# Three phases per step, two banks each for the score tiles, and the node columns read from an SBUF ring, in a graph layer with POOL-issued row moves

## The reference

```python
proj = einsum('ni,rio->nro', x, relation_weight)
t_r, h_r = proj[src, etype], proj[dst, etype]
att = sum(t_r * tanh(h_r + efeat), axis=-1)
a = segment_softmax(att, dst)
h_nb = segment_sum(x[src] * a[:, None], dst, n)
out = leaky_relu((x + h_nb) @ W.T, 0.01) + leaky_relu((x * h_nb) @ W2.T, 0.01)
return layernorm(x + out)
```

## Time and profile before

| | |
|---|---|
| median of 3 runs | 765.6 us |
| span of the profiled execution | 908.0 us |
| PE, DVE busy | 642.8 us, 608.1 us |
| POOL, ACT busy | 572.8 us, 514.2 us |
| DMA, mean | 77 GB/s |

### The profile page before, as it was taken

How to read it: one execution, slowest core, us unless ns; L and a number is a source line. 1 busy time by engine, 2 the same in 40 slices (tenths; PEclk the granted TensorE clock), 3 DMA queues, 4 the chain that set the end, 5 groups by cost and what they waited for, 6 DMA issues and landing times. The chain is left out here.

```text
span 908.0 us, 13811 instructions
## 1 busy us (share of the span) xinstructions
PE 642.8 (71%) x3948; PEld 356.0 (39%) x3948; DVE 608.1 (67%) x1094; ACT 514.2 (57%) x1457; POOL 572.8 (63%) x594
## 2 busy tenths in 40 slices
PE   2587778877777877877887876877788778865030
PEld 1434343544443443443443443343344344344020
DVE  2459768778778868869778769865686567754050
ACT  0255575577677667767677677744455244555052
POOL 7466666666666666666666666666666666666726
PEclk9788988798998998999897989879987889786555
DMA  5332432333332432432432421321111110000000
GB/s 139 107 101 71 115 103 81 114 103 81 115 103 81 116 104 69 127 103 67 128 104 60 123 81 45 104 73 64 50 48 43 62 57 28 27 29 28 24 6 17
DMA packets 48035, 70.37 MB, mean 77 GB/s; under 512 B 15971, under 2 KB 19487, under 8 KB 47959
## 3 DMA queue, kind: packets, MB, share of 16 engines
q1 hardware_dynamic: 18562, 32.97, 11.6%
q0 software_dynamic: 18752, 17.29, 9.1%
q10 hardware_dynamic: 10644, 19.23, 5.7%
HBM read 45.60 MB, written 25.78 MB: 79 GB/s over the span
## 5 line engine op out<-in xcount | busy, mean ns | idle before, releaser
L450 POOL DMA_INDIRECT xsd<-in_x,ends_i x388 | 378.4, 975 | 219.4 <-issue 91.1
L558 PE MATMUL t_ps<-xm,w_rel 64*64 64x512 f32 (+1 forms) x900 | 263.1, 682 | 17.7 <-DVE xm L996 9.2
L996 DVE SCALAR_TENSOR_TENSOR xm<-typ,xT_ps 128x1024 f32<-128x1024 f32 (+1 forms) x225 | 264.4, 1185 | 14.6 <-ACT xc L716 9.9
L560 PE MATMUL h_ps<-xm,w_rel 64*64 64x512 f32 (+1 forms) x900 | 264.3, 682 | 0.7 <-issue 0.4
L474 POOL DMA_INDIRECT out<-out_r,row_i x196 | 191.3, 976 | 110.4 <-issue 51.7
L575 PE MATMUL y_ps<-bd_cat,dT 128*128 128x256 f32 x392 | 127.0, 481 | 48.1 <-issue 28.6
L575 PEld LDWEIGHTS y_ps<-bd_cat,dT 128*128 128x128 f32 x392 | 89.3, 239 | 69.6 <-issue 33.8
L558 PEld LDWEIGHTS t_ps<-xm,w_rel 64*64 64x64 f32 x900 | 57.8, 149 | 118.4 <-issue 81.9
L740 ACT ACTIVATE o_t<-zd,rstd 128x64 f32<-128x64 f32 x392 | 98.8, 340 | 0.0
L585 PE MATMUL tr_ps<-ident,uw 128*128 128x128 f32 x196 | 35.9, 312 | 70.3 <-DVE uw L1090 31.9
L1058 DVE TENSOR_TENSOR zd<-rd,y_ps 128x512 f32<-128x512 f32 x49 | 33.4, 681 | 57.5 <-issue 29.8
(11 more groups left out here) (161 smaller groups left out, 982.8 us busy)
## 6 DMA issues: line engine op xcount, KB each, us to landing
x_in<-in_x SPq DMA_DIRECT2D x48, 256.0 KB
typ<-typ_d SPq DMA_DIRECT2D x24, 512.0 KB
out<-o_t ACTq DMA_DIRECT2D x48, 256.0 KB
xsd<-in_x SPq DMA_DIRECT2D x512, 0.2 KB
xsd<-in_x,ends_i POOLq DMA_INDIRECT x388
hist<-es ACTq DMA_DIRECT2D x24, 256.0 KB
ea<-in_edge_attr SPq DMA_DIRECT2D x24, 224.0 KB
out<-out_r,row_i POOLq DMA_INDIRECT x196
```

What stands on the lines that cost most here:

```text
L450: pool.indirect_dma_start(xsd[:, s % RX, j, side, :], None, x[:, :], bass.IndirectOffsetOnAxis(ap=ends_i[:, side, c:c + 1], axis=0),).then ...
L558: pe.matmul(t_ps[h * D:(h + 1) * D, 0:n], w[0:D, :], moving[0:D, h * n:(h + 1) * n], start=(at == 0), stop=(at == R - 1), skip_group_check ...
L560: mm = pe.matmul(h_ps[(1 - h) * D:(2 - h) * D, 0:n], w[D:P, :], moving[D:P, (1 - h) * n:(2 - h) * n], start=False, stop=(at == R - 1), ski ...
L996: v.scalar_tensor_tensor(xm[:, m % RM, 0:n], typ[:, s % RT, 0:n], float(r), xT_ps[:, 0:n], ALU.is_equal, ALU.mult).then_inc(masked, 1)
```

## The change

- `t_ps` and `h_ps` become two banks each (`t_two`, `h_two`), taken in turn by steps. `s_ps` goes; the scores lie in the step's own t bank, and the pair of step f is turned and multiplied in the two banks that rest, in halves instead of quarters.
- `xT_ps` shrinks to one bank. Its columns are turned in two halves of four, in the middle of the step before, and ACT copies each half to a ring `xc` of two buffers in SBUF (`columns_copy`, which replaces `plain`). All nine masks now read `xc`.
- The product of step e moves from the end of step e on DVE to step e+1, after its second mask; leaky and the two final additions move one step later.
- Quads signal only after numbers 2, 5 and 9 (`ENDS`), three phases a step; masks wait on phases.
- POOL's tie counts phases: one phase for each 7 moves, with a lead of 26 moves. `pe_marks` goes.
- The ring `out_r` has 17 buffers instead of 18. `dense_turn`, `dense_copy` and `dense_relu` stand at other places.

```diff
-RW = 18
-PACE, LEAD, PACE_OUT = 14.6, 250, 13.64
+RW = 17
+RC = 2
+PACE, LEAD, PACE_OUT = 7.0, 26, 7.0
...
+    ENDS = [2, 5, R - 1]
...
-        xc = sb("xc", [P, COLS * P])
+        xc = sb("xc", [P, RC, COLS * P])
...
-        xT_ps = ps("xT_ps", [P, COLS * P])
-        t_ps = ps("t_ps", [P, 512])
-        h_ps = ps("h_ps", [P, 512])
+        xT_ps = ps("xT_ps", [P, 512])
+        t_two = [ps(f"t_ps{i}", [P, 512]) for i in range(2)]
+        h_two = [ps(f"h_ps{i}", [P, 512]) for i in range(2)]
...
-        s_ps = ps("s_ps", [P, 512])
...
             def pace(n, scattered_blocks):
-                step_end = ends[min(NS - 1, RW + 4 + scattered_blocks)]
-                asked = min(n, G_MOVES[NS]) * PACE + max(n - G_MOVES[NS], 0) * PACE_OUT - LEAD
-                need = [k for k, (_, _, work) in enumerate(marks) if work <= min(asked, step_end)]
-                if need and need[-1] > at[0]:
-                    at[0] = need[-1]
-                    pool.wait_ge(marks[at[0]][0], marks[at[0]][1])
+                asked = min(int((min(n, G_MOVES[NS]) - LEAD) / PACE + max(n - G_MOVES[NS], 0) / PACE_OUT), len(ENDS) * (min(NS - 1, RW + 4 + scattered_blocks) + 1))
+                if asked > at[0]:
+                    at[0] = asked
+                    pool.wait_ge(quad_done, asked)
...
-            def plain(s):
-                n = cols(s) * P
-                act.wait_ge(xT_done, s + 1)
-                wait(act, quad_done, (s - 1) * R + PLAIN_AT + 1 if s > 0 else 0)
-                act.copy(xc[:, 0:n], xT_ps[:, 0:n]).then_inc(plain_done, 1)
+            def columns_copy(s, odd):
+                n = cols(s) // 2 * P
+                act.wait_ge(xT_done, 2 * s + odd + 1)
+                if s >= RC:
+                    act.wait_ge(masked, (s - RC + 1) * RB)
+                    act.wait_ge(quad_done, quads_until(s - RC, PLAIN_AT))
+                act.copy(xc[:, s % RC, odd * n:(odd + 1) * n], xT_ps[:, 0:n]).then_inc(xT_out, 1)
...
             def mask(s, r):
                 n = cols(s) * P
                 if r == 0:
-                    v.wait_ge(plain_done, s + 1)
+                    v.wait_ge(xT_out, 2 * s + 2)
                     v.wait_ge(typ_in[s % RT], turn(s, RT) * DMA)
                 m = s * RB + r
-                wait(v, quad_done, quad_count(m - RM) if m >= RM else 0)
-                v.scalar_tensor_tensor(xm[:, m % RM, 0:n], typ[:, s % RT, 0:n], float(r), xT_ps[:, 0:n],
+                wait(v, quad_done, mask_read(m - RM) if m >= RM else 0)
+                v.scalar_tensor_tensor(xm[:, m % RM, 0:n], typ[:, s % RT, 0:n], float(r), xc[:, s % RC, 0:n],
                                        ALU.is_equal, ALU.mult).then_inc(masked, 1)
```

More of the change, by code:

```diff
@@ L250, in o_need @@
             return sum(len(x_parts(d)) for d in mine) * DMA
[L252 to L299, removed]
-                paired(2)
-                turned(2)
-                quads(8, 9)
-                paired(3)
-                multiplied(2)
-                quads(9, 10)
-                if 0 <= s + 1 < NS:
-                    mark(xT_done, s + 2, 2 * cols(s + 1))
-                ends[s] = work[0]
-            return marks, ends
         block = ctx.enter_context(nc.Block())
@@ L824, in _ @@
-                if 0 <= s < NS:
-                    plain(s)
                 if D0 is not None:
                     dense_copy(D0)
-                if 0 <= f < NS:
-                    for g in range(groups(f)):
-                        heads(f, g)
+                if late and l < LATE:
+                    pair_out(l, 0)
+                if DP is not None:
+                    dense_relu(DP)
+                if late and l < LATE:
+                    pair_out(l, 1)
+                if ending:
+                    heads(f, 0)
@@ L831, in _ @@
+                if ending and groups(f) > 1:
+                    heads(f, 1)
+                if s == 0:
+                    act.copy(xfix[:, :], xsd[:, 0, 0, 1, :]).then_inc(xfix_done, 1)
                 for n in tiles(s - 2)[2:3]:
                     dense_norm(n)
+                for n in tiles(s - 2)[2:3]:
+                    store_o(n)
+                if more and s > 0:
+                    columns_copy(s + 1, 0)
+                if D1 is not None:
+                    dense_copy(D1)
@@ L1156, in _ @@
                 if on:
-                    score_max(e)
+                    product(e)
                 if main:
                     mask(s, 2)
+                if DP is not None:
+                    dense_add(DP)
+                if early:
+                    leaky(l)
+                if s == 1:
+                    tables()
+                if DP is not None:
+                    dense_total(DP)
+                if early:
+                    final_add(l)
+                if early:
+                    final_add_x(l)
+                if DP is not None:
+                    dense_centre(DP)
+                if ending:
+                    pair(f)
+                if main:
+                    mask(s, 3)
+                if on:
+                    score_max(e)
                 if on:
```

404 lines of the change are left out of this document (182 added, 222 removed).

## The result

The kernel after takes 855.28 us median (854.79 to 856.1, 4 runs), the kernel before 765.14 us beside it (762.71 to 766.09, 4 runs): ratio 1.1189, 95% interval 1.117 to 1.1207. It is 90 us slower; 840 was forecast, with a range of 752 to 862.

A forecast was written before the change was run, and what follows sets the result against it. The prediction took POOL's 586 moves to bound the kernel, with the compute chain close behind. It summed 753.4 (POOL alone) + 80 (masks) + 12.2 - 5 (waits that stay) to 840 us, range 752 to 862.

The forecast's parts named there:

- main case: POOL's 586 moves bound the kernel and masks reading `xc` hold them: 802 to 862 us, chance 0.72.
- POOL alone, 753.4: POOL's moves with their gaps and no real waits: profiled span 908.0 less 154.6 us of waits.
- Masks, 80: 225 DVE masks, now with two SBUF inputs, lengthen POOL moves that start in them: 80 us added.
- upper end of 102: Largest price of the masks' hold on POOL, with no drop in the pace of moves: 102 us.
- The formula: Masks' hold on POOL: 225 masks (9 half as long) x 0.57 / 1.45, 88 us.
- The rule: POOL moves starting in DVE operations of 0.68 us or more with two SBUF inputs lengthen by what is left less 0.12.
- Waits that stay, 12.2 - 5: POOL's waits for compute in the median run, at most 12.2 us, less about 5 gained at the tie's start.
- I give the compute side 60 to 120 us in the profiled execution: Gain on DVE, ACT and PE from two banks, later product and early columns, out of 157 us of overlapping waits.
- Masks don't hold POOL: Rival: masks with two SBUF inputs leave POOL's moves alone, so 760 us at POOL's floor; chance 0.06.
- the compute chain was the bound: Rival: POOL's moves are slower under the profiler and the freed compute chain counts: about 740 us; chance 0.13.
- The coarse tie: Rival: POOL waits for whole phases and falls back if compute stays at 30 us a step: near 790; chance 0.05.
- the first rival: Compute chain as bound: POOL alone 635 us plus 80 would hide under DVE's 702; about 740; chance 0.13.

The follow-up runs named there:

- Experiment 10: The kernel before with one operand changed, its masks reading `xc` in SBUF instead of `xT_ps`, at the level of 765: 854.39 us, ratio 1.1164.
- experiment 1: The kernel before with one operand changed, its masks reading `xc` in SBUF instead of `xT_ps`, at the level of 890: 914.41 us, ratio 1.029.
- experiment 11: The kernel before without its tie (POOL never waits for PE's quads), at the level of 765: 764.74 us, ratio 0.9999.
- experiment 9: The kernel after with each mask cut in four quarters, at the level of 765: 829.07 us, ratio 1.0813 to the kernel before.
- experiment 5: The kernel after again, unchanged, beside the kernel before at the level of 890: 940.68 us, ratio 1.0533.
- experiment 12: The kernel before with the tie of the kernel after (7 moves a phase, 26 ahead), at the level of 765: 765.01 us, ratio 0.9994.
- experiment 2: The kernel before without its tie (POOL never waits for PE's quads), at the level of 890: 1262.83 us, ratio 1.4199.

## Why the prediction was right, and where not

**The mechanism.** "POOL bound, and masks that read `xc` hold it" was the main case, at 0.72, and it is what happened. Experiment 10 isolates it. The page's sentence on two SBUF inputs that the prediction weighed (the Trainium skill, "SBUF — State Buffer", section "Who interferes with whom") agrees with these runs, also for indirect moves (experiments 1 and 10), but for the 29 that start together with a mask; the inference beside it, that such an operation leaves descriptor making alone, does not: it would have left experiment 10 at 765.

**The sum.** At the level of 765 it can now be made of measured terms. POOL without waits: 763.1 us of span (experiment 11). The longer moves: 669.1 - 577.8 = 91.3. Together 854.4, the span after. The time is 1.7 us above the span of the same execution (856.1 and 854.4; 764.78 and 763.1 in experiment 11). Against the terms of the prediction:

- *POOL alone, 753.4.* Measured 763.1. It was built from rows of the slower level. At 765 the two-input operations that were there before hold more, since the same work stands closer together: the four groups are busy 577.8 us, where the earlier trace rows had 571.7, 6.1 more. The other 3.6 are the gaps and the first wait (179.4 against 175.8).
- *Masks, 80.* This is the term that was mis-sized. The moves that start inside a mask are 100.2 us longer than plain ones, just under the upper end of 102. The formula gave 88, and I went below it because it overstated the small operations of before by a factor of two. That correction was wrong for masks. What falls is the other holding, by some 9 us, since fewer moves meet those operations; net 91.3. The rule, what is left less 0.12, has an error of 0.01 us at the median but isn't complete: 29 moves that start together with a mask pay nothing, some 33 us less than by the rule, and moves can be held through several operations in a row (experiments 9 and 10). The formula also takes the moves' starts as spread evenly, which they aren't. That it came within 12 us of 100.2 is partly luck.
- *Waits that stay, 12.2 - 5.* Measured none at either end. There were none before (experiment 11 has the same time without any tie), so neither the 12.2 nor the gain of 5 existed: the 12.2 are the 9.7 by which the floor was too low, the 1.7 between time and span, and 0.8 of scatter. That these 7.2 nearly made good for the floor is luck.
- The sum was 753.4 + 80 + 12.2 - 5 = 840.6. With its misses, 9.7 + 11.3 - 7.2 = 13.8, it is the span of 854.4; the median time lies 0.9 above.

**The 142.4 us between the profile and the median.** The prediction took the compute side to be slower in the profiled execution, with POOL waiting for it. That POOL's rows are the same in both was right. The reason was open, and it is not the profiler: unprofiled runs take 890 us on two chips. PE's signals come late there. The forecast of the profiled span, 850 to 890 and shorter than before, came true at 854.4 by luck. It was to come from the compute side getting faster and POOL's waits shrinking; what happened is that this execution was at the other level. At the level of the profile before, the kernel after has a span of 939.1 us (experiment 5).

**The compute side.** The step that failed is "I give the compute side 60 to 120 us in the profiled execution". The two profiles could not be compared: against the 908.0 us execution the masks of the kernel after end some 95 us earlier, but at its own level they end later. There was also less to gain: the three waits of the earlier trace rows, 157 us there, are 18.9 + 5.4 + 8.2 = 32.5 us in the kernel before at the level of 765 (experiment 11; experiment 12 has 18.9, 5.1 and 8.2). The last masks by source line, first of the kernel after, then of experiment 10 (count, then least, median and greatest duration in ns, then start of the first and of the last of them):

```profile
L930 DVE SCALAR_TENSOR_TENSOR xm<-typ,xc x5: 683/684/693, 715.1 to 722.2; 128x512 f32<-128x512 f32 x5
```

```profile
L996 DVE SCALAR_TENSOR_TENSOR xm<-typ,xc x5: 628/681/684, 645.7 to 653.4; 128x512 f32<-128x512 f32 x5
```

The last mask starts at 722.2 where it was 653.4. The rest of the change, banks, order and phases together, made the compute side about 69 us slower, and POOL hides it. The waits of the earlier trace rows did go, and others came. In the kernel after a mask waits 57.1 us in all (0.9 in experiment 10), and the longest of PE's waits in the stages is for the copy of the turned dense tile:

```profile
PE tr_ps L497 <- ACT dT L655: 68.6, 30, 5.5
```

Whether this new wait alone makes the difference was not tried. At the level of 890 the slower compute side isn't hidden: there the whole change costs 50 us, and its masks alone 24.

**Rivals.** "Masks don't hold POOL" fell with experiment 10, and "the compute chain was the bound" with experiment 11. The coarse tie was given 790: at the level of 765 it is worth nothing on the kernel before (experiment 12), where compute takes 27.6 us a step (447 - 33 over 15 steps, experiment 11) and not the 30 of the prediction's condition. The kernel after does take 30.0 us a step (483.8 - 34.2 over 15 steps), but its POOL, with the held moves at 1.46 us each, takes 30.7 for 21 of them and never waits. In experiment 9, with 30.6 us a step, POOL waits 34.1 us for the tie; what the kernel after would take without it at this level was not run. One slip in the first rival: its 635 + 80 = 715 lies above the 702 that it was to hide under.

## What to carry to other kernels

Where an engine issues indirect moves all the time, look for each DVE operation of 0.68 us or more beside them whose two tensor inputs both lie in SBUF, and keep one of them in PSUM: 225 masks moved from PSUM to SBUF made POOL's row 91 us longer, while two more banks had nothing to bring, since POOL waited for none of the others. Cutting such an operation in quarters gave back 59 us of the hold but cost DVE 45 us. And before a sum is made from a profile whose span is far from the median, find out whether the program has two levels: "remote" waits for PE all over the engines were the mark of the other one, and at that one the same edits are worth something else (the hold 24 instead of 88 us, the tie some 130 instead of none).

## What was not expected of the hardware

- On two of the four chips of the experiments PE's signals come late while POOL issues indirect moves, and PE itself pauses. With 39 to 41 moves per 50 us without a pause PE carries out 18 to 32 instructions in 50 us instead of some 300 (experiments 2 and 11: the same program takes 1262.83 and 764.74 us). With the fine tie it is about 1.4 us of mean lateness and 890 us instead of 765. Of DVE's and ACT's signals those that are recorded are not late (0.01 us at the median); in the 908.0 us execution, 430 of DVE's 1012 and 278 of ACT's 559 have no record. What in the chip couples the two, and why two chips show it and two don't, stays open: no run changed that alone.
- The granted TensorE clock fell after PE had slowed, so it does not make the levels. In the first 50 us of experiment 2 it was still 0.93 with PE busy for 11.6 us; from 50 to 100 us it was 0.57 with PE busy for 6.1, and from 150 us on 0.50, the lower level of 1.2 GHz. In experiment 11 it is 1.00 (2.4 GHz) from 50 to 100 us.
- A move that starts together with a mask escapes it. In the kernel after, 29 of the 30 that start in a mask's first 0.03 us take 0.94 to 0.97 us, and of the 7 that start 0.03 to 0.05 us into one, 6 take 2.00 to 2.03. In experiment 10 the first 0.03 us have 7 free and 7 held ones. No run shows why.
- Two-input operations without a gap between them can hold one move through all of them: 14 gathers of 2.71 us in experiment 10. It doesn't happen everywhere: most moves that start in an operation with another such one right behind it pay for the first alone, as in 7 of the 12 such gathers beside L1090 in experiment 1.
- A DVE operation cut in four keeps more of its hold than pieces of 0.3 us would: they take 417 ns each and start before the one ahead has ended, and 36 of 100 us stay on moves that start in a piece.
